# One signal on each product: the edge stage of a graph network on one Trainium2 core

## The chip, the core and the metric

The kernel runs on 1 of the 8 cores of a Trainium2 chip. The metric is the device time of one execution in microseconds (us); shown is the median of three runs. The engines are called by name: TensorE (matmul, PE in the profile; its weight loads are PEld), VectorE (DVE), ScalarE (ACT), GpSimd (POOL) and SyncE (SP), which only issues DMAs here. Each has its own queue of instructions, and they meet only at semaphores: an instruction adds to one when it is done ("carries a signal"), and another engine's wait passes once the count is reached.

## The reference

The input is x (1250 nodes, 512 features) and 40,000 edges sorted by target node. Four stages each add their result to x: a segment mean, a mixture of experts (8 experts, 2 of them per node), the edge stage of a graph network, and a second mixture of experts. The edge stage is the part that matters here:

```
x0, x1 = lin(x[:, :128], W_up0), lin(x[:, 128:] as (node, 128, 3), W_up1)
h = edge_attr_8
for W in (W_mlp1, W_mlp2, W_mlp3):
    h = 1.679177 * silu(h @ W / sqrt(rows of W))
w1, w2, w3, w4 = split(h @ W_mlp4 / sqrt(64), 4)          # 128 each, per edge
s0, s1 = x0[src], x1[src];  y0, y1 = edge_attr_4[:, :1], edge_attr_4[:, 1:]
m0 = concat(w1 * s0 * y0,  w4 * (s1 . y1) / sqrt(3))
m1 = concat((w2 * s0) y1,  w3 * s1 * y0)
msg0, msg1 = segment_sum(m0, dst), segment_sum(m1, dst)   # over the edges of a node
out = concat(lin(msg0, W_out0), lin(msg1, W_out1)) / 10
```

## The kernel before

The kernel is one program with an order written out by hand for each engine. Edges are packed into 352 tiles of 128 edges, so that the edges of 4 tiles (a step, Q = 4) fall on few target nodes; there are STEPS = 88 steps. A batch for the small network (the three silu layers) is 8 tiles, 44 batches.

In each step TensorE does this, in the loop over s at the end of the edge stage:
- weights_of (L1740): the last layer of the small network for each pair of tiles, four products of 64 rows each, two side by side in the array. Each product carries a signal (p_tp, "edge_weights").
- mlp_product: one or two layers of the small network, by the table of mlp_order. Layer 0 is one transpose (L1694), layer 1 four products (L1700), layers 2 and 3 four products each in quarters of the array (L1707). The last product of a layer carries the signal p_prod.
- sum_up, for the step before: 16 products that add the messages to the target nodes. For each c of 4 there are 4 products, one for each tile j, each in its own 32 columns of the array (128*32) and its own 32 partitions of PSUM. c = 0 (L1755, 512 elements wide) fills the first half of sum_pair, c = 1 to 3 (L1758, 256 wide) the second.

The signals of sum_up are these two lines:

```
                    if c == 0:
                        mm.then_inc(p_plain, 1)
                mm.then_inc(p_sum, 1)
```

p_plain rises once per step after the first half's last product, p_sum once after the second half's last.

Who waits for them:
- ScalarE, close(s): for each half it waits for the sum (p_plain, then p_sum), copies the half out of PSUM (L1402), and scales it in place (L1404) by a factor for each partition (g_same) before the next step adds to it. TensorE's next sum_up waits for that scaling (a_kept). SyncE writes the copy to HBM (L2128, three buffers).
- VectorE, messages_of (L1030 and L1032): the products of weights and gathered rows; it waits for the gather, for p_tp, and from step 2 on for p_sum of two steps before, since the message buffers are used again. Its signal v_msg lets TensorE's sum_up and its next weights_of start, and GpSimd's next gather.
- picks_of on VectorE (L1044) and ScalarE (L1389): selection matrices, three buffers, wait for p_sum of three steps before.
- ScalarE, mlp_function (L1321, L1325, L1329, L1333): the function after each layer; it waits for p_prod of that layer and of the layer of the batch before that read the buffer. Its signal a_mlp lets the next mlp_product start.
- GpSimd, gather (L1944): one indirect DMA per tile, 8 buffers, waits for v_msg.

The waits on p_prod count layers by their place in the order (mlp_place).

Of the kernel before, what the change touches and what calls it, by code (L numbers as in the profile page):

```python
# [41 lines left out]
Q = 4  # L42
BT = 8
NTILE = -(-((NE - NW) // TILE + NW) // BT) * BT
STEPS = NTILE // Q
NB = NTILE // BT
NREC = NTILE
# [93 lines left out]
def mlp_order():  # L141


    first = [(0, 0), (0, 1), (0, 2), (0, 3), (1, 1)]
    gaps = []
    for s in range(STEPS):
        r = s // 2 + 1
        a, b = ([(r, 2)], [(r, 3)]) if s % 2 == 0 else ([(r + 1, 0)] if r % 2 else [], [(r + 1, 1)])
        gaps.append([[x for x in g if x[0] < NB] for g in (a, b)])
    order = first + [x for g in gaps for x in g[0] + g[1]]  # L150
    return first, gaps, {x: n for n, x in enumerate(order)}


def program(nc, consts, x, anc, sub, leaf_table, src, dst, ea4, ea8, gate, w13, w2, w_up, w_mlp1, w_mlp23,
            w_mlp4, w_out, ew, ei, v1, v2, out):
    ctx = ExitStack()
    with ctx:
# [246 lines left out]

        mlp_first, mlp_gaps, mlp_place = mlp_order()

# [35 lines left out]
        def vector(v):  # L442
# [577 lines left out]
            def messages_of(s, h):  # L1020
# [6 lines left out]
                if s >= 2:  # L1027
                    v.wait_ge(p_sum, s - 1)
                weights = tp[:, :].rearrange("p (t w v u) -> p t w v u", t=2, w=2, v=2)
# [9 lines left out]
            def picks_of(s):  # L1039

                v.wait_ge(v_hot, s // HOT_STEPS + 1)
                if s >= NPICK:
                    v.wait_ge(p_sum, s - NPICK + 1)
                v.tensor_tensor(out=picks[s % NPICK][:, 0:VPICK],  # L1044
                                in0=hot[s // HOT_STEPS % NHOT][:, :, s % HOT_STEPS, 0:VPICK].rearrange(
                                    "p n j -> p j n").unsqueeze(2).to_broadcast([128, VPICK, 4, WN]),
                                in1=by_step[:, s, 0:VPICK, 2:6].unsqueeze(3).to_broadcast([128, VPICK, 4, WN]),
                                op=ALU.mult).then_inc(v_pick, 1)
# [31 lines left out]

            v.wait_ge(p_sum, STEPS)
            v.wait_ge(d_late, 64)
# [65 lines left out]
        def scalar(a):  # L1148
# [166 lines left out]
            def mlp_function(r, layer):  # L1315
                b = mlp_out[layer]
                a.wait_ge(p_prod, mlp_place[r, layer] + 1)
                if layer == 0:
                    if r:
                        a.wait_ge(p_prod, mlp_place[r - 1, 1] + 1)  # L1320
                    a.activation(out=fT, in_=b, func=ACT.Copy).then_inc(a_mlp, 1)  # L1321
                elif layer == 1:
                    if r:
                        a.wait_ge(p_prod, mlp_place[r - 1, 2] + 1)
                    a.activation(out=act1.rearrange("p (h x) -> p h x", h=2), in_=b, func=ACT.Silu, scale=8 ** -0.5).then_inc(a_mlp, 1)  # L1325
                elif layer == 2:
                    if r:
                        a.wait_ge(p_prod, mlp_place[r - 1, 3] + 1)
                    a.activation(out=act2.rearrange("p (h x) -> p h x", h=2), in_=b, func=ACT.Silu, scale=SILU_2MOM / 8).then_inc(a_mlp, 1)  # L1329
# [52 lines left out]
            def picks_of(s):  # L1382

                a.wait_ge(v_hot, s // HOT_STEPS + 1)
                if s >= NPICK:
                    a.wait_ge(p_sum, s - NPICK + 1)
                for j in range(VPICK, Q):
# [5 lines left out]
            def close(s):  # L1393
# [3 lines left out]
                if s == NSUM - 1:  # L1397
                    a.wait_ge(d_zero, 32)
                for h, ready in enumerate((p_plain, p_sum)):
                    half = slice(512 * h, 512 * (h + 1))  # L1400
                    a.wait_ge(ready, s + 1)
                    a.activation(out=run_sum[s % NSUM][:, half], in_=sum_pair[:, half], func=ACT.Copy).then_inc(a_out, 1)  # L1402
                    if s + 1 < STEPS:
                        a.activation(out=sum_pair[:, half], in_=sum_pair[:, half], func=ACT.Copy,  # L1404
                                     scale=g_same[:, s + 1:s + 2]).then_inc(a_kept, 1)
# [20 lines left out]
            def split_out(e):  # L1426
                if e:
# [6 lines left out]
                         scale=3 ** -0.5).then_inc(a_p4, 1)  # L1434
            a.wait_ge(p_sum, STEPS)
            a.wait_ge(a_out, 2 * STEPS)
# [34 lines left out]
        def tensor(pe):  # L1471
# [217 lines left out]
            def mlp_product(r, layer):  # L1689
# [3 lines left out]
                if layer == 0:  # L1693
                    mm = pe.transpose(out=b, in_=feat[:, r * 64:(r + 2) * 64], identity=ident)  # L1694
                elif layer == 1:
                    for k in range(2):
                        q = r % 2 * 2 + k
                        for h in range(2):
                            p = slice(64 * h, 64 * (h + 1))
                            mm = pe.matmul(out=b[:, h, k * 128:(k + 1) * 128], lhsT=m1_sb[p, q * 128:(q + 1) * 128],  # L1700
                                           rhs=fT[p], start=True, stop=True, skip_group_check=True)
                else:
                    w, given = (m23_sb[:, 0:HID], act1) if layer == 2 else (m23_sb[:, HID:2 * HID], act2)
                    for k in range(2):
                        for h in range(2):
                            p = slice(64 * h, 64 * (h + 1))
                            mm = pe.matmul(out=b[64 * k:64 * (k + 1), h], lhsT=w[p],  # L1707
                                           rhs=given[p, k * 256:(k + 1) * 256], start=True, stop=True,
                                           skip_group_check=True)
                mm.then_inc(p_prod, 1)  # L1710

# [31 lines left out]
            def sum_up(s):  # L1743
# [4 lines left out]
                for c in range(4):  # L1748
                    if s and c < 2:
                        pe.wait_ge(a_kept, 2 * s - 1 + c)  # L1750
                    for j in range(Q):
# [5 lines left out]
                        else:  # L1757
                            mm = pe.matmul(out=bank.rearrange("p (b u) -> p b u", b=4)[:, c - 1:4:4 - c], lhsT=pick,  # L1758
                                           rhs=m[:, 0:c + 5:c + 4], start=s == 0 and c == 1, stop=True,
                                           skip_group_check=True)  # L1760
                    if c == 0:
                        mm.then_inc(p_plain, 1)
                mm.then_inc(p_sum, 1)

# [440 lines left out]
```

## Time and profile before

| | |
|---|---|
| median of 3 runs | 1666.88 us (1664.09 to 1668.29) |
| the profiled execution | 1662.87 us |
| its span in the trace | 1660.9 us |
| TensorE busy in the span | 1433.7 us (86%) |
| VectorE, ScalarE, GpSimd busy | 1185.6, 940.7, 931.3 us |
| mean granted clock of TensorE, share of full | 0.935 |
| edge stage, 850 to 1525 us | 675 us |

The profiled execution is one execution, 4.0 us below the median of the runs. Its span begins with the first instruction and ends with the last. "Busy" is the time in which at least one instruction of the engine was at work. Ends of matmuls are modelled in the profile, starts are recorded. In the rows below "<-" names what released an engine after it stood idle; "remote" and "another core or an unknown queue" both stand for a releaser that the profile cannot name, here on one core.

### The profile page before, as it was taken

The page shows a single profiled execution, that of the slowest core. Times are in us where ns is not written, and L with a number is a line of the kernel's source. Part 1 is how long each engine was busy: PE and PEld are TensorE (multiplying, and loading weights), DVE is VectorE, ACT ScalarE, POOL GpSimd, SP SyncE. Part 2 cuts the span into 40 slices and gives each one's busy share as a digit, 9 for nine tenths or more (in the row PEclk, how much of TensorE's full clock was granted, in tenths as well). Part 3 has the DMA queues.
Part 4 walks back from the last instruction along what each step waited for, and adds up shares of the span by engine and source line. Part 5 has one row for each costly group of instructions (what it writes and reads, how often), then busy time and mean ns, then how long its engine had stood idle before and what let it go on. Part 6 is the DMA issues. An engine that isn't in the chain of part 4 may idle for free.

```text
span 1660.9 us, 24925 instructions
## 1 busy us (share of the span) xinstructions
PE 1433.7 (86%) x8774; PEld 850.1 (51%) x8774; DVE 1185.6 (71%) x1457; ACT 940.7 (57%) x1648; POOL 931.3 (56%) x762
## 2 busy tenths in 40 slices
PE   5949999999999999999677787877878787878999
PEld 3626658864887488748432232322323232334787
DVE  7887559963998399839757677676776676675565
ACT  6347558853887388738435554554554554554433
POOL 4155758888888887888145455455454455453100
PEclk9859999999999999999899899899898999899999
DMA  9255582695647657352566666666666666665421
GB/s 319 111 226 166 177 323 50 221 352 157 204 156 251 219 198 258 104 172 27 171 206 208 200 208 212 200 194 211 207 206 193 204 208 207 198 206 185 148 98 63
DMA packets 91603, 316.57 MB, mean 191 GB/s; under 512 B 23754, under 2 KB 25988, under 8 KB 80859
## 3 DMA queue, kind: packets, MB, share of 16 engines
q1 hardware_dynamic: 45832, 202.57, 32.8%
q0 software_dynamic: 45648, 112.41, 26.1%
q8 instruction: 71, 1.16, 0.3%
q14 instruction: 52, 0.43, 0.1%
HBM read 378.96 MB, written 77.16 MB: 275 GB/s over the span
## 4 chain that ended last, share of the span: by engine, by line
PE 52%; ACT 10%; POOL 9%; issue 9%; DVE 8%; another core or an unknown queue 8%; DMA 3%; DVEq 0%; SPq 0%; ACTq 0%; POOLq 0%
PE pair L1601 19%; POOL sorted_edges L1912 8%; PE pair L1758 5%; PE pair L1755 4%; PE pair L1740 4%; PE pair L1638 3%; ACT pair L1404 3%; PE pair L1851 3%; PE pair L1862 3%; PE pair L1707 2%; PE pair L1655 2%; DVE arena L1032 2%; ACT arena L1389 1%; PE pair L1592 1%
## 5 line engine op out<-in xcount | busy, mean ns | idle before, releaser
L1944 POOL DMA_INDIRECT arena<-node_table,arena x352 | 347.6, 987 | 359.7 <-DVE arena L1032 236.3
L1912 POOL DMA_INDIRECT sorted_edges<-arena x320 | 473.6, 1480 | 114.1 <-issue 100.2
L905 DVE TENSOR_TENSOR weights_hl<-arena,weights_hl 128x1024 fp32r<-128x1024 f32 x342 | 405.4, 1223 | 62.5 <-ACT weights_hl L1231 54.5
L1231 ACT ACTIVATE weights_hl<-arena 128x1024 fp32r<-128x1024 f32 x342 | 351.8, 1059 | 46.5 <-PE pair L1601 44.5
L1601 PE MATMUL pair<-weights_hl,rows_hl 128*128 128x512 f32 x1368 | 326.4, 396 | 4.7 <-ACT weights_hl L1231 3.0
L1032 DVE TENSOR_TENSOR arena<-pair,arena 128x1536 f32<-128x1536 f32 x176 | 307.3, 1746 | 0.0
L1601 PEld LDWEIGHTS pair<-weights_hl,rows_hl 128*128 128x128 f32 x1368 | 252.1, 189 | 70.4 <-DVE weights_hl L905 9.7
L1030 DVE TENSOR_TENSOR arena<-pair,arena 128x512 f32<-128x512 f32 x176 | 120.3, 684 | 205.0 <-PE pair L1740 104.4
L1402 ACT ACTIVATE arena<-pair 128x512 f32<-128x512 f32 x176 | 104.5, 594 | 219.9 <-remote 150.5
L1740 PE MATMUL pair<-arena 64*128 64x512 f32 x704 | 191.2, 629 | 37.3 <-DVE arena L1032 31.3
L1758 PE MATMUL pair<-arena 128*32 128x256 f32 x2112 | 163.5, 430 | 4.3 <-issue 4.1
L1601 PE MATMUL pair<-weights_hl,hidden_hl 128*128 128x512 f32 x684 | 165.7, 395 | 0.0
L1758 PEld LDWEIGHTS pair<-arena 128*32 128x32 f32 x2112 | 79.7, 125 | 121.5 <-issue 96.6
L1601 PEld LDWEIGHTS pair<-weights_hl,hidden_hl 128*128 128x128 f32 x684 | 124.9, 188 | 25.6
L1740 PEld LDWEIGHTS pair<-arena 64*128 64x128 f32 x704 | 60.9, 189 | 116.3 <-issue 87.9
L924 DVE TENSOR_TENSOR arena<-pair,arena 128x512 f32<-128x512 f32 x69 | 47.3, 685 | 98.2 <-PE pair L1638 53.5
L1404 ACT ACTIVATE pair<-pair,arena 128x512 f32<-128x512 f32 x174 | 114.5, 658 | 0.0
L1755 PE MATMUL pair<-arena 128*32 128x512 f32 x704 | 112.2, 714 | 0.1
L1269 ACT ACTIVATE arena<-pair 128x512 f32<-128x512 f32 x69 | 41.4, 600 | 98.4 <-PE pair L1638 70.5
L1389 ACT ACTIVATE arena<-arena 128x32 f32<-128x32 bf16 x352 | 94.6, 345 | 0.0
L1707 PE MATMUL pair<-arena 64*64 64x256 f32 x704 | 61.3, 416 | 31.5 <-ACT arena L1325 29.6
L1638 PE MATMUL pair<-arena 128*64 128x512 f32 x352 | 86.6, 601 | 0.4 <-DMA arena<-in_w 0.2
(287 smaller groups left out, 1578.2 us busy)
## 6 DMA issues: line engine op xcount, KB each, us to landing
arena<-in_w SPq DMA_DIRECT2D x73, 2048.0 KB
arena<-in_w SPq DMA_DIRECT2D x85, 1024.0 KB
sums<-arena SPq DMA_DIRECT2D x88, 512.0 KB
other_down<-in_w SPq DMA_DIRECT2D x8, 1024.0 KB
arena<-in_v SPq DMA_DIRECT2D x16, 512.0 KB, 4.4
pair_rows<-arena SPq DMA_DIRECT2D x1, 5934.0 KB
arena<-pair_rows SPq DMA_DIRECT2D x23, 256.0 KB
arena<-node_table,arena POOLq DMA_INDIRECT x352
```

The lines of the kernel that those rows point to most:

```text
L905: v.tensor_tensor(out=part[s][:, 1], in0=by_chunk(n)[4], in1=part[s][:, 0].bitcast(F32), op=ALU.subtract).then_inc(v_low, 1)
L1030: v.tensor_tensor(out=m[:, :, 0:2], in0=weights[:, :, :, 1], in1=rows_in[:, :, 0:1].to_broadcast([128, 2, 2, MUL]), op=ALU.mult)
L1032: v.tensor_tensor(out=m[:, :, 2:8].rearrange("p t b u -> p t (b u)"), in0=weights[:, :, :, 0].rearrange("p t w u -> p (t w) u").unsqueeze( ...
L1231: a.activation(out=part[s][:, 0], in_=cols, func=ACT.Copy).then_inc(a_high, 1)
L1404: a.activation(out=sum_pair[:, half], in_=sum_pair[:, half], func=ACT.Copy, scale=g_same[:, s + 1:s + 2]).then_inc(a_kept, 1)
L1601: mm = pe.matmul(out=bank[:, :], lhsT=st[:, a], rhs=part[s][:, w, half * 512:(half + 1) * 512], start=begins and (a, w) == (0, 0), stop=en ...
L1638: mm = pe.matmul(out=banks[2 + 2 * s + c][HALF * h:HALF * (h + 1), :], lhsT=xS[:, at:at + HALF], rhs=w[:, c], start=k == 0, stop=k == 3, s ...
L1740: pe.matmul(out=tp_bank[(i + h) % Q], lhsT=act3[batch % 2][p, k * 128:(k + 1) * 128], rhs=m4_sb[p], start=True, stop=True).then_inc(p_tp, 1)
L1755: mm = pe.matmul(out=bank, lhsT=pick, rhs=m[:, 1:5], start=s == 0, stop=True, skip_group_check=True)
L1758: mm = pe.matmul(out=bank.rearrange("p (b u) -> p b u", b=4)[:, c - 1:4:4 - c], lhsT=pick, rhs=m[:, 0:c + 5:c + 4], start=s == 0 and c == ...
L1912: g.indirect_dma_start(out=sorted_edges, out_offset=bass.IndirectOffsetOnAxis(ap=slot_i[:, j:j + 1], axis=0), in_=er[:, j, :], in_offset=N ...
L1944: g.indirect_dma_start(out=row, out_offset=None, in_=table, in_offset=bass.IndirectOffsetOnAxis(ap=senders[:, i:i + 1], axis=0)).then_inc( ...
```

## The change

Every product of sum_up and every product of a layer of the small network now carries a signal, and all waits on p_sum, p_plain and p_prod count the products. Step s has 4 signals on p_plain and 12 on p_sum (SUMS = 3 * Q); mlp_order returns a second table, mlp_done, with the number of products up to and including each layer (1 for layer 0, 4 for the others). The order of instructions is the same as before on all engines, with the same 3774 instructions in TensorE's order. The other waits of the same kind as those shown change alike.

```diff
+SUMS = 3 * Q
...
     order = first + [x for g in gaps for x in g[0] + g[1]]
-    return first, gaps, {x: n for n, x in enumerate(order)}
+    done = dict(zip(order, itertools.accumulate(1 if layer == 0 else 4 for _, layer in order)))
+    return first, gaps, {x: n for n, x in enumerate(order)}, done
...
                 if s >= 2:
-                    v.wait_ge(p_sum, s - 1)
+                    v.wait_ge(p_sum, SUMS * (s - 1))
...
                 if s >= NPICK:
-                    v.wait_ge(p_sum, s - NPICK + 1)
+                    v.wait_ge(p_sum, SUMS * (s - NPICK + 1))
...
                 b = mlp_out[layer]
-                a.wait_ge(p_prod, mlp_place[r, layer] + 1)
+                a.wait_ge(p_prod, mlp_done[r, layer])
                 if layer == 0:
                     if r:
-                        a.wait_ge(p_prod, mlp_place[r - 1, 1] + 1)
+                        a.wait_ge(p_prod, mlp_done[r - 1, 1])
...
-                for h, ready in enumerate((p_plain, p_sum)):
+                for h, (ready, each) in enumerate(((p_plain, Q), (p_sum, SUMS))):
                     half = slice(512 * h, 512 * (h + 1))
-                    a.wait_ge(ready, s + 1)
+                    a.wait_ge(ready, each * (s + 1))
...
                 if layer == 0:
-                    mm = pe.transpose(out=b, in_=feat[:, r * 64:(r + 2) * 64], identity=ident)
+                    pe.transpose(out=b, in_=feat[:, r * 64:(r + 2) * 64], identity=ident).then_inc(p_prod, 1)
                 elif layer == 1:
...
-                            mm = pe.matmul(out=b[:, h, k * 128:(k + 1) * 128], lhsT=m1_sb[p, q * 128:(q + 1) * 128],
-                                           rhs=fT[p], start=True, stop=True, skip_group_check=True)
+                            pe.matmul(out=b[:, h, k * 128:(k + 1) * 128], lhsT=m1_sb[p, q * 128:(q + 1) * 128],
+                                      rhs=fT[p], start=True, stop=True, skip_group_check=True).then_inc(p_prod, 1)
                 else:
...
-                            mm = pe.matmul(out=b[64 * k:64 * (k + 1), h], lhsT=w[p],
-                                           rhs=given[p, k * 256:(k + 1) * 256], start=True, stop=True,
-                                           skip_group_check=True)
-                mm.then_inc(p_prod, 1)
+                            pe.matmul(out=b[64 * k:64 * (k + 1), h], lhsT=w[p],
+                                      rhs=given[p, k * 256:(k + 1) * 256], start=True, stop=True,
+                                      skip_group_check=True).then_inc(p_prod, 1)
...
-                    if c == 0:
-                        mm.then_inc(p_plain, 1)
-                mm.then_inc(p_sum, 1)
+                        mm.then_inc(p_sum if c else p_plain, 1)
```

## Rows read from the trace of the kernel before

**Rows 1.** The page: span.
```profile
span 1660.9 us, 24925 instructions
```

**Rows 2.** Windows, edge stage: us, busy by engine, PEclk, DMA share, GB/s.
```profile
850.00:1525.00 675.00, 530.69 (x4551) 200.10 (x4551) 473.03 (x456) 357.51 (x848) 341.06 (x346) 0.90 0.65 203
```

**Rows 3.** Instructions of lines L1755, L1758, L1740: ns min/median/max, first and last start.
```profile
L1755 PE MATMUL pair<-arena x704: 590/617/1063, 852.5 to 1519.7; 128*32 128x512 f32 x176
...
L1758 PE MATMUL pair<-arena x2112: 376/379/634, 854.2 to 1521.2; 128*32 128x256 f32 x192
...
L1740 PE MATMUL pair<-arena x704: 586/589/1216, 834.5 to 1513.6; 64*128 64x512 f32 x176
```

**Rows 4.** Waits, edge stage: us in total, times, longest us.
```profile
ACT arena L1402 <- remote: 150.5, 49, 6.0
...
DVE arena L1030 <- remote: 91.7, 27, 3.6
```

**Rows 5.** Timeline from 999.6 us: start, us, engine line op, [idle before <-releaser].
```profile
999.68 1.26 PE L1758 MATMUL pair<-arena 128*32 128x256 f32 x20
...
1000.41 0.95 POOL L1944 DMA_INDIRECT arena<-node_table,arena  x1 [0.49 <-issue]
...
1000.88 0.66 PE L1707 MATMUL pair<-arena 64*64 64x256 f32 x8
...
1001.47 2.21 PE L1740 MATMUL pair<-arena 64*128 64x512 f32 x8
...
1004.24 0.96 POOL L1944 DMA_INDIRECT arena<-node_table,arena  x1 [0.30 <-issue]
1006.37 0.60 ACT L1402 ACTIVATE arena<-pair 128x512 f32<-128x512 f32 x1 [5.04 <-remote]
1006.71 0.69 DVE L1030 TENSOR_TENSOR arena<-pair,arena 128x512 f32<-128x512 f32 x1 [3.55 <-remote]
...
1008.49 1.94 PE L1755 MATMUL pair<-arena 128*32 128x512 f32 x8
```

**Rows 6.** Timeline from 1508.8 us, behind the stage's last gathers.
```profile
1508.88 1.06 PE L1755 MATMUL pair<-arena 128*32 128x512 f32 x8
...
1509.51 0.96 POOL L1944 DMA_INDIRECT arena<-node_table,arena  x1 [0.30 <-issue]
...
1514.16 1.06 PE L1755 MATMUL pair<-arena 128*32 128x512 f32 x8
...
1515.04 1.48 PE L1758 MATMUL pair<-arena 128*32 128x256 f32 x24
1515.35 0.60 ACT L1402 ACTIVATE arena<-pair 128x512 f32<-128x512 f32 x1 [1.65 <-PE pair L1755]
...
1516.58 0.60 ACT L1402 ACTIVATE arena<-pair 128x512 f32<-128x512 f32 x1
```

**Rows 7.** Windows, one microsecond behind the wait of rows 5.
```profile
1007.00:1008.00 1.00, 0.00 (x0) 0.00 (x0) 1.00 (x2) 1.00 (x2) 0.00 (x0) 0.50 0.37 152
```

**Rows 8.** Chain that ended last: shares in the edge stage, then pieces from 1001 us.
```profile
by line: another core or an unknown queue 19.6%; PE pair L1758 13.4%; issue 13.0%; PE pair L1755 10.7%; PE pair L1740 8.9%; ACT pair L1404 7.9%; PE pair L1707 4.6%; DVE arena L1032 4.5%; ACT arena L1389 3.6%; ACT arena L1402 3.0%; DVE arena
...
1001.32 5.02 another core or an unknown queue
1006.34 0.02 issue
...
1006.39 0.05 another core or an unknown queue
...
1013.65 0.02 issue
...
1014.82 0.31 another core or an unknown queue
...
1022.40 0.03 issue
...
1022.59 0.69 DVE arena L1030
```

More of the change, by code:

```diff
@@ L403, in program @@
         v_co, p_y, v_y = sem("coefficients"), sem("second_out"), sem("second_added")
-        mlp_first, mlp_gaps, mlp_place = mlp_order()
+        mlp_first, mlp_gaps, mlp_place, mlp_done = mlp_order()
         def by_chunk(n):
@@ L1079, in split_out @@
                                 op=ALU.subtract).then_inc(v_w2, 1)
-            v.wait_ge(p_sum, STEPS)
+            v.wait_ge(p_sum, SUMS * STEPS)
             v.wait_ge(d_late, 64)
@@ L1323, in mlp_function @@
                     if r:
-                        a.wait_ge(p_prod, mlp_place[r - 1, 2] + 1)
+                        a.wait_ge(p_prod, mlp_done[r - 1, 2])
                     a.activation(out=act1.rearrange("p (h x) -> p h x", h=2), in_=b, func=ACT.Silu, scale=8 ** -0.5).then_inc(a_mlp, 1)
@@ L1327, in mlp_function @@
                     if r:
-                        a.wait_ge(p_prod, mlp_place[r - 1, 3] + 1)
+                        a.wait_ge(p_prod, mlp_done[r - 1, 3])
                     a.activation(out=act2.rearrange("p (h x) -> p h x", h=2), in_=b, func=ACT.Silu, scale=SILU_2MOM / 8).then_inc(a_mlp, 1)
@@ L1385, in picks_of @@
                 if s >= NPICK:
-                    a.wait_ge(p_sum, s - NPICK + 1)
+                    a.wait_ge(p_sum, SUMS * (s - NPICK + 1))
                 for j in range(VPICK, Q):
@@ L1434, in scalar @@
                          scale=3 ** -0.5).then_inc(a_p4, 1)
-            a.wait_ge(p_sum, STEPS)
+            a.wait_ge(p_sum, SUMS * STEPS)
             a.wait_ge(a_out, 2 * STEPS)
```

## Prediction

> **What bounds the kernel now.** I read the page's slices first, then the edge stage as one window, then who waits for whom in it, then the order of time in two of its steps, then the chain. The edge stage runs from about 850 to 1525 us of a span of 1660.9 [rows 1, 2]: 675 us for 88 steps. The first sum products of the first and last step start at 852.5 and 1519.7 us [rows 3], so a step takes 667.2 / 87 = 7.7 us. No engine fills it: TensorE is busy 531 us, VectorE 473, ScalarE 358, GpSimd 341, the DMA engines 65% [rows 2]. What fills the rest is waiting in a circle. TensorE's sum products release ScalarE (close), ScalarE's scaling in PSUM releases the next sum, VectorE's messages release both the next weights and the next gathers. The reader should see in [rows 4] that ScalarE's copy L1402 stands 150.5 us for a releaser that the profile cannot name ("remote") in 49 places, and VectorE's L1030 91.7 us in 27.
>
> [Rows 5] show one such place. The twelve L1758 products end at 999.68 + 1.26 = 1000.94 us, but the copy that waits for them starts at 1006.37. TensorE meanwhile went on with L1707 and L1740 and had finished at 1003.68; VectorE, which waits for L1740, starts at 1006.71. So TensorE's signals arrived late, all of them together, with the work long done. I call this a hold. GpSimd issued gathers (L1944) all through it, the last from 1004.24 to 1005.20. [Rows 6] show the opposite: after the last gathers (1509.51) L1755 ends at 1515.22 and its copy starts at 1515.35, L1758 ends at 1516.52 and its copy starts at 1516.58; a step there is 1514.16 - 1508.88 = 5.3 us. A hold also costs clock: TensorE stands still, and afterwards it is granted 0.50 [rows 7], the lower level, at which the four L1755 products take 1.94 us instead of 1.06 [rows 5, 6]. On the stage's chain the unnamed releaser has 19.6% [rows 8], 0.196 x 675 = 132 us, or 26 holds of the 5.02 us of [rows 8].
>
> **The change, part by part.** No instruction is added, removed or moved on any engine; no queue and no DMA is touched. What is added is signals: 14 per step on sum products (16 instead of 2), 88 x 14 = 1232, and 3 for each of layers 1 to 3 of 44 batches of the small network, 396; together 1628. [Rows 3] show a product as two matmul records (2112 for 1056 products at L1758). The waits ask for all signals of a group, so each passes at its last one, as before. The wait cannot pass earlier; it passes later by what three more signals cost, since the four products of a group run side by side and end together.
>
> *Price of a signal.* L1740's products carry one each already and run at full pace: eight records in 2.21 us, two side by side, 589 ns median each [rows 3, 5]. So a signal does not slow a product; the price is only in the tail where several end together. No row isolates it. The nearest is the end of the hold. The copy starts at 1006.37, its signal arrived 0.03 before (the "issue" piece of [rows 8]), at 1006.34. VectorE starts at 1006.71, and it needs 0.19 us from a signal to the start (1022.40 to 1022.59 in [rows 8]), so its signal arrived at 1006.52. In those 0.18 us TensorE reported six products, four of L1707 with one signal and two of L1740 with two. If signals alone cost time, one costs 0.06 us; if products alone do, an added signal costs nothing. I take the middle, 0.03.
>
> The Trainium skill (TensorE: Matmul & The Clock Gate, section "The cost: per-tile semaphore tail") says that signals of side-by-side products serialise, 26.3 ns each, and that one on the last is enough because products end in program order. By its figure the tails below would be 0.08 us where I have 0.09, an estimate; it speaks against this change.
>
> *Tails.* Three added signals make 0.09 us at each wait that the end hangs on. In the 22 us of chain in [rows 8] there are three steps and four such passes: the copies at 1006.34 and 1013.65, and the network's ScalarE pieces after 1006.39 and 1014.82. That is 1.33 per step, 117 in the stage, 117 x 0.09 = 10.5 us. Upper bound: every one of the 3.5 waits a step (two sums, 1.5 network layers) on the path at 0.06 a signal, 308 x 0.18 = 55 us. Lower bound 0.
>
> *Queue behind a hold.* During a hold the signals wait in line, and now there are more of them ahead of VectorE's: up to 11 of the sum, 3 of L1707, so 14 x 0.03 = 0.42 us, of which 0.18 is in the tails already. 26 x 0.24 = 6 us if all twelve products are caught. In [rows 5] only the last ones can be, since the first end before the first gather at 1000.41; I take half, 3 us. Bounds 0 and 26 x 14 x 0.06 = 22 us.
>
> *Signals on layer products outside a hold.* Four L1707 products end before L1740's; L1740 takes 2 us, which hides 0.09. If that cover went, it would be in the bound above. The other stages are unchanged: 0.
>
> Sum: 10.5 + 3 = 13.5, say 14 us. The profiled execution took 1662.87 us, so 1676.9; the median of the runs is 4.0 above it, so 1681 us (+0.8%). A measurement of this kernel can tell about 0.3%, 5 us, from no change.
>
> **The rivals.**
> *Covered.* The tails fall inside waits that something else ends. For it: a hold ends at about the same moment for the copy and for VectorE, whenever TensorE had finished, so what is late by 0.1 us inside it costs nothing, and ScalarE's copy stands 150.5 us in holds [rows 4]. Against it: the four passes of [rows 8] are on the chain. Then 0 to 4 us: 1667 to 1671 us.
>
> *The holds give way.* Holds are seen behind groups in which only the last of four to twelve products signals (L1758, L1707), and their cause is not known to me. If what is stuck is the report of products without a signal, signals on all let it out. It decides by whether the "remote" rows of [rows 4] shrink. All holds gone would be 132 us, 1535; half of them 66 us, 1601. The same sign comes from a mere shift of phase: a step takes 5.3 us where no gathers meet it and 7.7 on the mean, and 0.1 us may move the meeting for the better. Against it: L1740's products all signal and are held as well [rows 5].
>
> *The holds spread.* If it is the signals that cannot get through while GpSimd issues gathers, then 16 instead of 2 a step have to get through, and TensorE itself may stop when too many wait. Its place is c = 1 to 3 of sum_up, 12 signals in 1.3 us; it decides once a hold comes more often than now, 26 in 88 steps. One in every second step would be 44, 18 more at 5.02 us: +90 us, 1757. For it: the holds lie under gathers, and [rows 6] have none. Against it: L1740's signals in [rows 5] arrive in one burst, so once open the way takes many.
>
> The Trainium skill (VectorE: DVE Perf Modes, its warning on the event accelerator) says that dense signals from several engines should be spaced out, as they can even lock one another. By it a slower or stopped stage is the likelier of these two; no row here shows a lock.
>
> That the change does not do what it says is excluded: the order of instructions is the same on all engines, and each counted total (4 per step for the first half, 12 for the second, 4 per layer) matches the signals given.
>
> **How the numbers follow.** Tails and queue, 1672 to 1722: 0.47. Covered: 0.17. Holds give way or the phase shifts well: 0.24. Holds spread: 0.12. So faster by over 0.3% 0.24, within 0.3% 0.17, slower 0.59. The time is that of the likeliest, 1681. The range has to hold 8 in 10: down to 1635 it takes in the smaller half of the gains (0.12 left out), up to 1745 the sum of the bounds (1667 + 77 = 1744) and part of the spreading (0.07 left out). The forecast's own range is 1672 to 1722.
>
> **What would show it.** Right: edge stage 10 to 20 us longer, the "remote" rows of ScalarE and VectorE near 150 and 92 us, the copy of L1755 starting 0.2 us after its end instead of 0.13 in the gather-free steps, GpSimd, VectorE and DMA busy times unchanged. Wrong: the "remote" waits fall by tens of us and the granted clock of the stage rises from 0.90 (the holds give way), they grow by tens (they spread), or the stage's length does not move (covered).

## The result

Twenty runs of each kernel: 1670.70 us median after (1660.9 to 1684.9), 1665.64 before (1660.71 to 1675.88). The ratio is 1.0037, 95% interval 1.0021 to 1.0053: slower by 5 us between the medians, or 6 by the ratio, where 14 were forecast. The profiled execution took 1673.44 us, its span is 1671.4 us.

The edge stage in the changed kernel, as one window (us, busy time by engine in the order PE, PEld, DVE, ACT, POOL, then granted clock, share of the DMA engines, GB/s):

```profile
850.00:1535.00 685.00, 536.95 (x4551) 202.28 (x4551) 474.08 (x457) 357.19 (x848) 341.38 (x346) 0.90 0.64 200
```

Instruction counts are those of [rows 2] but for one of VectorE's; VectorE, ScalarE and GpSimd are busy as long as before within 1.1 us, TensorE 6 us longer, and the clock is the same 0.90. The window is 10 us longer than that of [rows 2], by choice of its end, and no engine has more instructions to do. Lines have moved by one or two: L1402 is now L1404, L1030 is L1032, L1755 and L1758 are L1756 and L1759, L1740 is L1741, L1944 is L1943. The sum products, by line (duration in ns min/median/max, first and last start in us):

```profile
L1756 PE MATMUL pair<-arena x704: 589/617/1062, 853.4 to 1529.9; 128*32 128x512 f32 x176
...
L1759 PE MATMUL pair<-arena x2112: 376/379/634, 855.1 to 1531.4; 128*32 128x256 f32 x192
```

Medians are those of [rows 3] and the longest agree within 1 ns: a product that signals is no slower. From the first start to the last the first half's products now take 676.5 us instead of 667.2. The waits of the stage:

```profile
ACT arena L1404 <- remote: 140.7, 48, 5.1
DVE arena L1032 <- PE pair L1741: 118.9, 41, 6.7
...
DVE arena L1032 <- remote: 86.4, 24, 3.8
```

The line of VectorE's named wait was, in the kernel before:

```profile
DVE arena L1030 <- PE pair L1740: 104.4, 37, 5.1
```

Beside [rows 4], the unnamed waits are not longer (140.7 for 150.5, 86.4 for 91.7), but VectorE's named one is: 118.9 for 104.4. Both of VectorE's together are 205.3 for 196.1, 9.2 us more, as much as the stage's 9.3. The holds are neither gone nor more frequent here: the second half's signal comes over 3 us behind its products in 22 steps before and in 23 now, 5.4 us behind them in the mean of both. (In another group the unnamed waits of the changed kernel were much longer; see the experiments.) One hold, with the step behind it, in order of time:

```profile
1003.18 1.48 PE L1759 MATMUL pair<-arena 128*32 128x256 f32 x24
...
1004.59 0.66 PE L1709 MATMUL pair<-arena 64*64 64x256 f32 x8
1005.18 2.20 PE L1741 MATMUL pair<-arena 64*128 64x512 f32 x8
...
1007.95 0.95 POOL L1943 DMA_INDIRECT arena<-node_table,arena  x1 [0.30 <-issue]
1010.19 0.60 ACT L1404 ACTIVATE arena<-pair 128x512 f32<-128x512 f32 x1 [5.08 <-remote]
1010.61 0.69 DVE L1032 TENSOR_TENSOR arena<-pair,arena 128x512 f32<-128x512 f32 x1 [3.75 <-remote]
...
1012.31 1.94 PE L1756 MATMUL pair<-arena 128*32 128x512 f32 x8
...
1014.45 0.60 ACT L1404 ACTIVATE arena<-pair 128x512 f32<-128x512 f32 x1 [0.79 <-PE pair L1756]
...
1017.50 1.88 PE L1741 MATMUL pair<-arena 64*128 64x512 f32 x8
1017.58 0.60 ACT L1404 ACTIVATE arena<-pair 128x512 f32<-128x512 f32 x1 [1.98 <-PE pair L1759]
...
1019.11 0.60 ACT L1327 ACTIVATE arena<-pair 128x512 f32<-128x512 f32 x1 [0.38 <-PE pair L1702]
1019.37 0.69 DVE L1032 TENSOR_TENSOR arena<-pair,arena 128x512 f32<-128x512 f32 x1 [3.37 <-PE pair L1741]
...
1020.35 1.06 PE L1756 MATMUL pair<-arena 128*32 128x512 f32 x8
```

And the same step before, which [rows 5] left at 1008.49:

```profile
1010.55 0.60 ACT L1402 ACTIVATE arena<-pair 128x512 f32<-128x512 f32 x1 [0.71 <-PE pair L1755]
...
1013.46 1.89 PE L1740 MATMUL pair<-arena 64*128 64x512 f32 x8
1013.67 0.60 ACT L1402 ACTIVATE arena<-pair 128x512 f32<-128x512 f32 x1 [1.97 <-PE pair L1758]
...
1015.16 0.60 ACT L1325 ACTIVATE arena<-pair 128x512 f32<-128x512 f32 x1 [0.34 <-remote]
1015.41 0.69 DVE L1030 TENSOR_TENSOR arena<-pair,arena 128x512 f32<-128x512 f32 x1 [3.32 <-PE pair L1740]
...
1016.40 1.07 PE L1755 MATMUL pair<-arena 128*32 128x512 f32 x8
```

Counted from the copy that ends the hold (1006.37 before, 1010.19 after), the reader can lay the two side by side. VectorE's first messages: 0.34 and 0.42 us. The first half's products: 2.12 and 2.12. The first half's copy: 4.18 and 4.26. The second's: 7.30 and 7.39. The weights L1740: 7.09 and 7.31. The network's function (L1325, now L1327): 8.79 and 8.92. The next step's products: 10.03 and 10.16. So the tail of 0.08 us is there at both copies, but only 0.13 us of all that reaches the next step. The trace tells the same of the other steps. These are four of them, the 12th to the 15th, each from one start of the second half's products to the next (us):

| | with the long hold | the step behind it | third | fourth |
|---|---|---|---|---|
| before | 10.79 | 7.05 | 4.83 | 8.45 |
| after | 10.80 | 7.24 | 4.84 | 8.44 |

The tails are in all four; the time shows them in one. In 17 places both traces have a hold of over 5 us in the same step. There the step with the hold and the one behind it are 0.20 us longer together in the mean (from 0 to 0.5), 3.5 us in all. Behind the last gathers the tail stands alone:

```profile
1519.11 1.06 PE L1756 MATMUL pair<-arena 128*32 128x512 f32 x8
...
1524.39 1.06 PE L1756 MATMUL pair<-arena 128*32 128x512 f32 x8
...
1525.27 1.48 PE L1759 MATMUL pair<-arena 128*32 128x256 f32 x24
...
1525.66 0.60 ACT L1404 ACTIVATE arena<-pair 128x512 f32<-128x512 f32 x1 [1.52 <-PE pair L1756]
```

The products end at 1525.45, the copy starts at 1525.66, 0.21 us later, where [rows 6] have 0.13: three more signals, 0.08 us. The step before it is as long as before the change: 1524.39 - 1519.11 = 5.28 us, and 1514.16 - 1508.88 = 5.28 in [rows 6].

Why the holds did not change can now be read from the trace's semaphore records, since each product leaves one. These are the signals of the second half (p_sum), of the network (p_prod) and of the weights (p_tp) in the hold above; the first number is the time in us, and one record of p_sum is missing:

```
1004.280 p_sum   1004.323 p_sum   1005.042 p_sum   1005.779 p_sum   1005.821 p_sum
1007.230 p_sum   1007.973 p_sum   1008.697 p_sum   1008.739 p_sum
1010.125 p_sum   1010.168 p_sum
1010.210 p_prod  1010.253 p_prod  1010.295 p_prod  1010.338 p_prod
1010.380 p_tp    1010.423 p_tp    1010.465 p_tp    1010.508 p_tp
```

A hold is no full stop. The prediction took it for one ("all of them together"). While GpSimd issues its gathers the products of sum_up are reported one or two at a time, 0.7 or 1.4 us apart, and all that is left comes in a burst, 0.043 us apart, 1.2 us behind the end of the last gather's row (1007.95 + 0.95 = 1008.90). With one signal in twelve one sees only the last of them. Before, that last one came 5.40 us after the modelled end of L1758 (1000.94 to 1006.34), now 5.51 us (1004.66 to 1010.17). Over all the long holds the mean is 5.40 us before and 5.38 now. So the length of a long hold did not depend on how many of the products signal. The short ones did grow: reports 1 to 3 us late are in 18 steps before and in 29 now. Most of these are third steps like those of the table (late by 1.35 us where it was 0.65), and those are no longer for it.

### The profile page after: what moved, and what is told of

It is laid out like the page before. It is cut to its first block, busy times and chain, and to the rows that moved or that the text cites. A ratio compares the mean times of both kernels' runs of the same rounds, so it can differ in the third digit from the quotient of the medians.

```text
span 1671.4 us, 24925 instructions
## 1 busy us (share of the span) xinstructions
PE 1440.2 (86%) x8774; PEld 852.8 (51%) x8774; DVE 1185.5 (71%) x1457; ACT 940.6 (56%) x1648; POOL 929.5 (56%) x762
## 4 chain that ended last, share of the span: by engine, by line
PE 41%; POOL 17%; issue 12%; ACT 11%; another core or an unknown queue 8%; DVE 7%; DMA 3%; SPq 0%; DVEq 0%; ACTq 0%; POOLq 0%
POOL sorted_edges L1911 15%; PE pair L1603 11%; PE pair L1759 7%; PE pair L1756 4%; ACT pair L1406 4%; PE pair L1850 3%; PE pair L1861 3%; PE pair L1741 2%; PE pair L1640 2%; PE pair L1709 2%; ACT arena L1391 2%; POOL node_sums L1921 2%; DVE arena L1034 1%; PE pair L1657 1%
## 5 line engine op out<-in xcount | busy, mean ns | idle before, releaser
L1943 POOL DMA_INDIRECT arena<-node_table,arena x352 | 347.0, 986 | 369.7 <-DVE arena L1034 245.4
L1032 DVE TENSOR_TENSOR arena<-pair,arena 128x512 f32<-128x512 f32 x176 | 120.4, 684 | 214.2 <-PE pair L1741 118.9
L1404 ACT ACTIVATE arena<-pair 128x512 f32<-128x512 f32 x176 | 104.4, 593 | 218.3 <-remote 140.7
L1741 PE MATMUL pair<-arena 64*128 64x512 f32 x704 | 191.7, 629 | 37.5 <-DVE arena L1034 30.6
L1759 PE MATMUL pair<-arena 128*32 128x256 f32 x2112 | 166.9, 440 | 5.2 <-issue 3.3
L1759 PEld LDWEIGHTS pair<-arena 128*32 128x32 f32 x2112 | 81.2, 127 | 124.4 <-issue 98.3
L1741 PEld LDWEIGHTS pair<-arena 64*128 64x128 f32 x704 | 60.8, 188 | 118.5 <-issue 94.9
L1756 PE MATMUL pair<-arena 128*32 128x512 f32 x704 | 113.8, 724 | 0.0
```

The lines of the kernel that those rows point to most:

```text
L1741: pe.matmul(out=tp_bank[(i + h) % Q], lhsT=act3[batch % 2][p, k * 128:(k + 1) * 128], rhs=m4_sb[p], start=True, stop=True).then_inc(p_tp, 1)
L1756: mm = pe.matmul(out=bank, lhsT=pick, rhs=m[:, 1:5], start=s == 0, stop=True, skip_group_check=True)
L1943: g.indirect_dma_start(out=row, out_offset=None, in_=table, in_offset=bass.IndirectOffsetOnAxis(ap=senders[:, i:i + 1], axis=0)).then_inc( ...
```

## The experiments

Kernels in one group ran on one chip, beside runs of the kernel before there. There are five groups; the record numbers their chips 13, 5, 10, 10 and 13. Ratios are to these, with 95% intervals. The edits are to the kernel before unless said otherwise.

**The two halves of the change.** sum_only is the changed kernel with the network's signals put back to one a layer, net_only the changed kernel with the sum's put back to two a step.

```diff
-SUMS = 3 * Q
+SUMS = 1
...
-                        mm.then_inc(p_sum if c else p_plain, 1)
+                    if c == 0:
+                        mm.then_inc(p_plain, 1)
+                mm.then_inc(p_sum, 1)
```

(This is net_only; sum_only takes back the p_prod lines instead.)

> Signals on all 16 sum products, the small network as before (one signal a layer). Theory tails: each added signal costs 0.027 us at the end of a group of four, and most of the measured +0.37% (6 us) comes from the sum, whose signals are 1232 of 1628: ratio 1.002 to 1.003, edge stage 4 to 7 us longer. Rival queue ahead of the weights: what costs is the network's three extra signals in front of the weights' signals, then this run is within 0.1% of before.

> Signals on all products of the small network, the sum as before (two signals a step). Theory tails: ratio 1.000 to 1.001. Rival queue ahead of the weights: ratio 1.003 to 1.004, the whole of the change.

Measured: sum_only 1666.58 us, 1.0113 (1.0068 to 1.0159); net_only 1666.26 us, 1.0101 (1.0056 to 1.0145). The kernel before had 1649.5 us here, in runs from 1638.92 to 1664.17. Neither theory: each half costs 1%, more than the whole cost in the first comparison (0.4%) and nearly as much as it cost in the next group (1.2%). Across groups, then, the parts do not seem to add, as terms "so many signals at such a price" would have to; the whole did not run in this group.

**Without the gathers.** Only the first 8 of the 352 gathers are made, with one signal and with all.

```diff
             def gather(i):
+                if i >= NGAT:
+                    return
...
-                    v.wait_ge(d_gat[(first + t) % NGAT], 16 * ((first + t) // NGAT + 1))
+                    v.wait_ge(d_gat[(first + t) % NGAT], 16)
```

> The kernel before, but of the 352 gathers only the first 8 are made, and VectorE uses those rows again and again (left out: the rows of the other 344 tiles). If the gathers make the holds: the unnamed waits of the copy and of the messages (150 and 92 us) fall below 10 us, steps take about 5.3 us, the stage about 470 us instead of 667, the whole about 1470 us. If holds belong to the products themselves: unnamed waits stay above 100 us and the time stays above 1600 us.

> The changed kernel with the same 344 gathers left out. Theory tails: with no holds, only the tails are left; 0.08 us at each wait on the path. One such wait per step gives 7 us, two give 14 us over the run with one signal. Rival covered: the two are within 2 us, since without gathers VectorE's 5.3 us a step is the bound and TensorE's tails lie beside it.

Measured: 1466.14 us (1462.82 to 1467.52) with one signal, 1465.63 us (1464.39 to 1467.09) with all. The window of no_gather_one's edge stage:

```profile
856.00:1326.00 470.00, 458.52 (x4538) 178.36 (x4530) 465.81 (x454) 347.56 (x844) 1.24 (x2) 1.00 0.24 99
```

There is no unnamed wait left in the stage, VectorE is busy 466 of 470 us and bounds it, and the clock is 1.00. Without gathers and holds the kernel is 183 us faster than the kernel before in this group. And 1628 added signals cost nothing that shows: VectorE waits for its weights not once with one signal and once, 2.3 us, with all, so the tails are covered.

**What in a gather makes the hold.** plain_one fetches as many bytes by ordinary DMAs from SyncE at the same points, plain_all does so with all signals. small_one keeps GpSimd's indirect DMAs and fetches an eighth of the bytes.

```diff
-            for i in range(NTILE):
-                gather(i)
...
+                        if n >= NGAT:
+                            s.wait_ge(v_msg, n - NGAT + 1)
+                        s.dma_start(out=gat_pair[n % NGAT // 2][:, n % 2].rearrange("p m u -> p (m u)"),
+                                    in_=table[NP * (n % 9):NP * (n % 9 + 1)]).then_inc(d_gat[n % NGAT], 16)
```

> The kernel before, but the 352 gathers are ordinary DMAs of 128 table rows in a row, issued by SyncE at the same points (left out: the choice of the rows). Bytes and waits stay, GpSimd issues nothing in the stage. If GpSimd's issue of indirect DMAs makes the holds: unnamed waits below 10 us, stage 470 to 520 us, whole 1470 to 1520 us. If the gathers' traffic into SBUF makes them: unnamed waits above 80 us, stage above 600 us.

> The changed kernel with the same ordinary DMAs. If the signals cost only where gathers hold them: within 2 us of plain_one. If tails cost 0.08 us on the path wherever there is one: 5 to 14 us more.

> The kernel before, but each of the last 344 gathers brings 64 elements a row instead of 512 (left out: the rest of the rows, and the right choice of them). GpSimd issues as many indirect DMAs as before, an eighth of the bytes. If GpSimd's issue makes the holds: unnamed waits within 20% of 150 and 92 us, time above 1620 us. If the traffic makes them: unnamed waits below 30 us, about 1480 us.

> The changed kernel itself, once more, on one chip with the kernel before. Twenty runs of each gave a ratio of 1.0037; the two halves alone gave 1.0113 and 1.0101 on another chip, whose kernel before was faster (1649.5 us). If the halves' numbers were a chip's, this gives 1.000 to 1.012 with the same spread of 10 us and more between runs; if the parts really cost 1% each and partly cancel, it stays at 1.004.

Measured, in one group: plain_one 1466.11 us, plain_all 1466.39 us, small_one 1655.52 us (1.0008, 0.9976 to 1.0039), all_signals 1672.84 us (1.0121, 1.0082 to 1.0159), the kernel before 1651.86 us. The window of plain_one's stage and the waits of small_one's:

```profile
855.00:1328.00 473.00, 460.64 (x4539) 178.77 (x4532) 466.05 (x453) 348.21 (x845) 1.93 (x2) 1.00 0.84 287
```

```profile
ACT arena L1402 <- remote: 148.9, 35, 6.0
...
DVE arena L1030 <- remote: 100.8, 30, 3.7
```

The full traffic into the same buffers, at 287 GB/s and with no GpSimd, makes no hold; GpSimd's indirect DMAs with little traffic make all of it. So in these runs it is not the bytes that hold TensorE's reports but GpSimd's indirect DMAs. What in them does it (the engine's work at the issue, or the fetching of rows chosen one by one) these runs do not separate, since plain_one changes both. The changed kernel had its usual time, but the kernel before was 14 us faster here than in the first comparison, which makes 1.2% out of 0.4%. Its unnamed waits were not the usual ones:

```profile
ACT arena L1404 <- remote: 190.5, 56, 6.0
...
DVE arena L1032 <- remote: 115.7, 34, 3.7
```

That is 40 and 15 us more than the most in any trace of the kernels with one signal at each wait (150.5 and 100.8), and the prediction had named growth by tens of us as the sign that holds spread. Yet holds of over 3 us at the second half are 22, as before. What differs is the rhythm: from the 15th step on most long steps take 11.9 us, not 10.8, and the four steps of a round 31.9 us (11.9, 7.2, 6.9, 5.9). The trace of net_only (160.6 and 107.3 us) has nearly the same. The long steps are not the signals' doing: small_one beside it has them too, at 11.8 to 11.9 us, in rounds of about 30 and 31.5 us. But no trace of the kernel before was kept in either of these two groups, so how much of the rest is the signals' doing stays open.

**How much of the signals, and where.** before_again is the kernel before itself. last_group signals on the four products of c = 3, early_groups on c = 1 and 2 and the very last, plain_tail on the four of c = 0; the network is as before in all.

```diff
+                        if c in (1, 2) or c == 3 and j == Q - 1:
+                            mm.then_inc(p_sum, 1)
```

(early_groups, with SUMS = 9; the first half signals once, as before.)

> The kernel before, unchanged, run as if it were a change: what the comparison itself can tell. Expected 1.000, interval about 0.4% each way. If it is over 1.005 away from 1, the 1% of the single parts is no effect of the signals.

> Only the last four sum products (c = 3) signal on their own, the rest as before: 3 added signals a step, all of them in the tail of p_sum. Theory tails: 0.08 us at p_sum on the path in some steps, ratio 1.001 to 1.003. Rival pattern (a small delay anywhere tips the meeting of steps and gathers): as much as all signals, 1.010.

> The eight products of c = 1 and 2 signal and the last one of c = 3, the rest as before: 8 added signals a step, none in a tail. Theory tails: 1.000. Rival queue (signals drain slowly under gathers and stand ahead of later ones): as much as all signals or more than last_group, 1.005 to 1.012, and longer unnamed waits.

> Only the four products of c = 0 signal on their own: 3 added signals a step in the tail of p_plain. Theory tails: the copy of the first half starts 0.21 us after the products' end instead of 0.13 where nothing holds it, and the scaling behind it is on the path in the step after a hold: ratio 1.001 to 1.003. Rival pattern: 1.010.

Measured: before_again 1.0019 (0.9987 to 1.0051), last_group 1.0041 (1.0012 to 1.0070), early_groups 1.0041 (1.0009 to 1.0072), plain_tail 1.0022 (0.9990 to 1.0054). The runs of the kernel before, 35 of them, lie between 1635.75 and 1679.82 us. The null run is 0.2% off by itself, so the difference between 3 signals in a tail and 8 outside it cannot be told here. What it does say: no small part of the signals brings a full per cent here.

**Signals, or any delay?** With the parts not adding, I suspected the four-step rhythm: steps of about 10.8, 7.0, 4.8 and 7.8 us follow one another for most of the stage (from one start of L1758 to the next), and any small delay might tip it. late_copy puts a delay on ScalarE in front of both copies and adds no signal.

```diff
                     a.wait_ge(ready, s + 1)
+                    a.activation(out=cells[:, 2 * s + h:2 * s + h + 1], in_=ones[:, 0:1], func=ACT.Copy)
                     a.activation(out=run_sum[s % NSUM][:, half], in_=sum_pair[:, half], func=ACT.Copy).then_inc(a_out, 1)
```

> The changed kernel once more, on a third chip. If the effect is one number, 1.004 to 1.012 with the kernel before at 1650 to 1665 us and this one again near 1671 us.

> The kernel before with a one-element copy on ScalarE before each of its two copies of the sum (left out: nothing; added: some 0.2 us of ScalarE per copy, no signal). Theory rhythm: any delay in the circle of TensorE, ScalarE and gathers lengthens the four-step cycle, so this costs as much as all signals or more: ratio 1.008 to 1.03. Rival signals: only signals held under gathers cost; ScalarE's 0.2 us lie in its idle time: ratio below 1.003.

> The kernel before, but the four gathers of a step start only when the sum of two steps earlier is reported (p_sum). Theory: a step has some 5 us of gather issue in which TensorE reports slowly; starting them behind the sum takes the sum's signals out of it, so the longest unnamed waits (5 to 6 us) go and the time falls to 1600 us or less. Rival: the gathers then come too late for VectorE and the stage gets longer, 1680 us or more.

> As plain_one (rows by ordinary DMAs), and GpSimd issues 344 indirect scatters of 14 elements a row at the moments at which it issued the gathers (left out: the choice of the rows). If the issue of any indirect DMA holds TensorE's signals: unnamed waits above 80 us and about 1650 us. If only gathers do: about 1466 us as plain_one.

after_sum lets the first gather of a step also wait for p_sum; scatter is plain_one with indirect scatters on GpSimd.

```diff
                     g.wait_ge(v_msg, i - NGAT + 1)
+                    if i % Q == 0 and i >= NGAT:
+                        g.wait_ge(p_sum, i // Q - 1)
```

Measured: in this group the kernel before itself took 1460.27 us (23 runs, 1458.03 to 1463.70). Nothing in it had been changed; its gathers ran as ever, and there were no holds. The changed kernel took 1462.71 us, 1.0010 (1.0001 to 1.0020). Its stage:

```profile
849.00:1325.00 476.00, 459.70 (x4535) 178.80 (x4528) 465.67 (x452) 348.49 (x842) 336.72 (x342) 1.00 0.87 285
```

GpSimd is busy 337 us with the gathers as before, and yet the clock is 1.00 and no wait is unnamed. So GpSimd's gathers are needed for a hold (the groups above) and not enough for one: something outside the kernel, which these runs do not show, decides. It was the same throughout a group, and it is not the chip alone: the record has number 10 for this group and for the one before it, where the kernel before took 1650.95 us. It also gives the price of the tails where gathers run but hold nothing: 1.5 to 2.4 us (0.1% of 1460, and the difference of the medians), with an interval that just clears no change. late_copy cost 1.0018 (1.0004 to 1.0032) here. after_sum took 1747.1 us: VectorE now waited for gathers that came too late,

```profile
DVE arena L1030 <- DMA arena<-node_table,arena: 250.0, 53, 8.7
```

which is the rival's outcome, but without holds it says nothing on whether the holds could be dodged this way. scatter took 2207.26 us, because I made each scatter wait for the one before to land; with that and with no holds in the group it answers nothing, and whether scatters hold as gathers do stays open.

**The same pair once more, with holds.** Kernels as above.

> The kernel before with a one-element copy on ScalarE before each of its two copies of the sum, once more: in the call before, the kernel before itself showed no holds (1460 us) and this cost 0.2%. If there are holds this time (before near 1650 us): theory rhythm 1.005 to 1.03, rival signals below 1.003. If there are none again: 1.002.

> The changed kernel beside it, for the same call. With holds: 1.004 to 1.012, and about as much as late_copy_2 if any delay does it. Without holds: 1.001, as in the call before.

Measured: late_copy_2 1663.98 us, 0.9998 (0.9982 to 1.0015); all_third 1671.92 us, 1.0045 (1.0028 to 1.0063); the kernel before 1664.19 us (22 runs). The holds were back:

```profile
ACT arena L1402 <- remote: 130.9, 44, 5.1
```

The added copy is no trifle, and it sits where the signals' tail sits. From its own timeline in steps without a gather:

```profile
1521.89 0.20 ACT L1402 ACTIVATE arena<-arena 128x1 f32<-128x1 f32 x1 [1.56 <-PE pair L1756]
1521.99 0.58 ACT L1403 ACTIVATE arena<-pair 128x512 f32<-128x512 f32 x1
```

The real copy starts 0.10 us later than it would, more than the 0.08 us of three signals, at both halves of every step, and costs nothing that shows. So in this group the rhythm theory falls in the form "any delay in the circle": ScalarE's, before its copies, does not count. It is the signals at TensorE that cost the 0.4%, and where there are no holds they cost 0.1% or nothing that shows. Two gaps stay. The added copy does not delay what the network's signals delay, the functions and VectorE's weights, and net_only cost 1%. And it never ran in a group where the kernel before took 1650 us, in which the cost was 1% and more.

## Why the prediction was wrong

**The picture of the stage held.** Holds, gathers above them, no engine full, products unslowed, 19.6% of the chain on an unnamed releaser: the changed kernel shows 19.7%.

```profile
by line: another core or an unknown queue 19.7%; PE pair L1759 17.0%; issue 13.5%; PE pair L1756 10.0%; ACT pair L1406 8.6%; PE pair L1741 5.2%; ACT arena L1391 4.8%; PE pair L1709 4.7%; ACT arena L1404 3.0%; DVE arena L1034 2.9%; ACT arena
```

**The price of a signal held.** "I take the middle, 0.03" measured 0.08 us for three, 0.027 each. The records of the burst show it as well: the network's four products (the last report of the sum to the network's last) took 1006.437 - 1006.344 = 0.093 us with one signal and 1010.338 - 1010.168 = 0.170 with four. Reports with a signal stand 0.043 us apart, but one without a signal took time too, so the added price is less than that. The Trainium skill (TensorE: Matmul & The Clock Gate, "The cost: per-tile semaphore tail") has 26.3 ns, and the trace agrees. The copy behind the first half starts 0.21 us after the products, as announced.

**The step that failed is "Tails"**: 1.33 passes a step on the path, 117 in the stage, 10.5 us. What the trace showed in its place is 0.20 us for each long hold and nothing in the third and fourth steps. The tail is real at each pass (4.26 for 4.18, 7.39 for 7.30) but rarely reaches the next step. I had counted a pass as on the path because the chain goes through it, in 22 us of chain that began inside a hold. The chain names what came last; it does not say that the next thing would come earlier without it. Where nothing is held VectorE's work is the bound, so the tails cost nothing that shows (no_gather pair: -0.5 us, plain pair: +0.3 us, both within the spread) or up to 2.4 us (the group at 1460 us). Under holds, the 17 that compare one by one gave 3.5 us; at 0.20 us each, all 22 would give 4.5, an estimate. The profiled stage is 9.3 us longer. 1.8 us of it is in the first three steps (3.2 in the first alone, of which the next two give back 1.4), and the rest is in places where the steps fell into another order, as around the 30th, 53rd and 63rd. One execution does not tell whether these belong to the change. Where the 5 to 6 us between the runs come from is therefore shown only in part: signals under holds, 3.5 us of the profiled execution's, in the steps with a long hold and behind them.

**"Queue behind a hold", 3 us**: VectorE's start moved from 0.34 to 0.42 us behind the copy, 0.08 us, by the network's three signals ahead of it; nearly all of the sum's had already trickled out during the hold, which I had half allowed for. The term was small in either case.

**The rivals.** "The holds spread" rested on signals having to squeeze through, each for itself. The semaphore records show the pace per product, and the signals ride on it; long holds are 22 to 24 in each of the three traces of the changed kernel that have holds, against 22 before. But the sign that was to show it, unnamed waits longer by tens of us, did appear in the second group (190.5 and 115.7 us), so there the rival is not ruled out. "The holds give way" fell the same way: all products signal and are held as before. "Covered" was the nearest to the truth. The measured 1670.70 us lies in its 1667 to 1671, though in part by luck, since the kernel before measured 1665.64 and not the 1666.88 of its three runs. It holds wherever nothing is held; in the three groups with holds in which the whole change ran, 0.4 to 1.2% is beyond it.

**The yardstick moved too.** With holds the changed kernel took 1670.70, 1672.84 and 1671.92 us in three groups; the kernel before took 1665.64, 1651.86 and 1664.19 us. Between groups the kernel before differs by 14 us and the changed kernel by 2. The steps show a difference: in before_again four steps take 29.5 us at first and then mostly between 28 and 32, with long steps of 11.9 us; in the profiled run of the first comparison most take 30.4 to 31.2, with long steps of 10.8. What sets the rhythm I cannot say. It is not the chip alone: on number 13 the kernel before took 1649.5 us in one group and 1664.19 in another. That each half of the change alone gave 1% fits a picture in which either half pushes the kernel out of the short rhythm. Their kept traces fit it too (net_only: four steps in 31.6 us for most of the stage; sum_only: 30.7), but with no trace of the kernel before beside them it was argued, not tested.

## What to carry to other kernels

A signal on each product cost 0.027 us where several ended together; before that is put on the bill, ask which engine would be early if the wait passed sooner. A wait whose releaser the profile cannot name while TensorE has long ended is worth more attention than the waits with names: here it stood for some 185 us, and two kernels that left the indirect gathers out, or replaced them, showed it at once. And where a stage runs in a rhythm of several steps, compare at several times and on several chips, with the kernel before beside each, or the ratio is that of one group. Keep a trace of the kernel before in each group too; two questions here stay open for want of one.

## What was not expected of the hardware

- While GpSimd issued indirect DMAs, TensorE's completed products were reported one or two at a time, 0.7 to 1.4 us apart, for up to 6 us. So it was in the first comparison and in four of the five later groups (kernel before at 1649.5 to 1665.6 us). The same bytes by SyncE's DMAs: no hold. An eighth of the bytes by GpSimd: the same hold.
- In the earlier stages GpSimd issues 320 indirect scatters beside full-array products; the unnamed waits there are 0.4 us in all.
- In one group the same kernel ran some 190 us faster than in the group before it on the same chip number, 1460 us in 23 of 23 runs (1650.95 in 35), with the same gathers.
- After 20 of the 22 long holds of the kernel before, TensorE's granted clock fell to 0.50, the lower of its two levels, for 3.4 or 6.8 us; without holds it was 1.00 over the stage, against 0.90.
- In a burst, the report of a product with a signal came 0.043 us behind the one before it, and three added signals made the wait for a group of four 0.08 us longer.
